# Attention in two transformer layers: heads in order, the maximum pass on 32-row strips of the PE array

## The reference

```
scores = jnp.einsum('bhqd,bhkd->bhqk', q, k) / jnp.sqrt(jnp.float32(HEAD_DIM))
scores = jnp.where(causal[None, None], scores, -jnp.inf)
attn = jax.nn.softmax(scores, axis=-1)
out = jnp.einsum('bhqk,bhkd->bhqd', attn, v)
x = x + ga * (out @ W_o)
```

## Time and profile before

| | |
|---|---|
| median of three runs | 1506.66 us |
| span of the profiled execution | 1517.5 us |
| attention of layer 0 (first maximum tile to the last output tile) | 109.8 to 602.8 us |
| attention of layer 1 | 815.9 to 1306.0 us |
| PE busy over the span | 1211.4 us, 80% |
| DVE busy over the span | 951.7 us, 63% |
| ACT busy over the span | 683.7 us, 45% |

### The profile page before, as it was taken

How to read it: one execution, slowest core, us unless ns; L and a number is a source line. 1 busy time by engine, 2 the same in 40 slices (tenths; PEclk the granted TensorE clock), 3 DMA queues, 4 the chain that set the end, 5 groups by cost and what they waited for, 6 DMA issues and landing times. The chain is left out here.

```text
span 1517.5 us, 20983 instructions
## 1 busy us (share of the span) xinstructions
PE 1211.4 (80%) x7346; PEld 524.4 (35%) x7347; DVE 951.7 (63%) x2598; ACT 683.7 (45%) x895; POOL 187.9 (12%) x257
## 2 busy tenths in 40 slices
PE   2917999999799998319553899999989999676984
PEld 2502333333233343207421223233333334444663
DVE  6627888888678772301163788888868775342443
ACT  1302465665566666103230445566656667421331
POOL 4110000000000000344410000000000000054442
PEclk9857999999899999559875899999999999777997
DMA  4154000230502000022216310140120000011113
GB/s 128 31 118 68 16 16 15 39 74 16 67 15 73 3 3 1 22 63 57 76 50 123 52 43 19 35 87 25 26 44 2 3 3 2 1 35 43 47 47 104
DMA packets 41740, 64.10 MB, mean 42 GB/s; under 512 B 5440, under 2 KB 27872, under 8 KB 41328
## 3 DMA queue, kind: packets, MB, share of 16 engines
q1 hardware_dynamic: 37328, 53.95, 16.4%
q0 software_dynamic: 4320, 8.92, 1.7%
HBM read 45.55 MB, written 18.92 MB: 42 GB/s over the span
## 5 line engine op out<-in xcount | busy, mean ns | idle before, releaser
L792 ACT ACTIVATE probs_at<-st 128x1024 f32<-128x1024 f32 (+3 forms) x640 | 545.7, 897 | 382.4 <-PE st L747 236.4
L810 DVE TENSOR_REDUCE mxp_at<-mx 128x1 f32<-128x512 f32 x768 | 498.4, 685 | 96.0 <-PE mx L716 95.1
L716 PE MATMUL mx<-ks,qs 128*128 128x512 bf16 (+3 forms) x1280 | 379.9, 368 | 84.9 <-DVEq L801 33.2
L747 PE MATMUL st<-qs,ks 128*128 128x512 bf16 (+3 forms) x1280 | 355.6, 354 | 13.9 <-DMA qs<-shrow_at 12.6
L812 DVE CUSTOM_DVE_ANT_0 junk_at<-mx,maskN 128x384 f32<-128x384 f32 (+3 forms) x512 | 241.2, 485 | 104.7 <-PE mx L716 102.4
L763 PE MATMUL av<-probs_at,vs 128*32 128x512 f32 (+3 forms) x2560 | 301.7, 543 | 0.2
L716 PEld LDWEIGHTS mx<-ks,qs 128*128 128x128 bf16 x1280 | 104.8, 98 | 437.7 <-DVE mxp_at L810 183.6
L747 PEld LDWEIGHTS st<-qs,ks 128*128 128x128 bf16 x1280 | 123.4, 99 | 111.0 <-ACT probs_at L792 21.8
L1027 POOL DMA_INDIRECT perm<-rows,pos x64 | 63.3, 989 | 512.6 <-SPq L1136 248.4
L750 PE MATMUL st<-maskTb,identb 128*128 128x128 bf16 x512 | 100.9, 222 | 0.0
L763 PEld LDWEIGHTS av<-probs_at,vs 128*32 128x32 f32 x2560 | 50.6, 108 | 107.2 <-issue 96.7
(11 more groups left out here) (232 smaller groups left out, 1027.8 us busy)
## 6 DMA issues: line engine op xcount, KB each, us to landing
qs<-q_parts SPq DMA_DIRECT2D x63, 128.0 KB
ks<-k_parts SPq DMA_DIRECT2D x18, 384.0 KB
w_sb<-in_w_dram SPq DMA_DIRECT2D x16, 256.0 KB, 3.1
q_parts<-part_pj SPq DMA_DIRECT2D x12, 256.0 KB, 3.0
k_parts<-part_pj SPq DMA_DIRECT2D x12, 256.0 KB, 4.7
perm<-in_pad_dram SPq DMA_DIRECT2D x1, 2600.0 KB, 11.6
rows_f<-perm SPq DMA_DIRECT2D x39, 65.0 KB, 1.8
ks<-k_parts SPq DMA_DIRECT2D x12, 192.0 KB
```

Of the source, the lines that this page charges most:

```text
L716: pe.matmul(buf[:, 0:w], QS[p][:, j, (4 * Q + qb) * P:(4 * Q + qb + 1) * P], KS[p][:, j, c * CH:c * CH + w], start=True, stop=True).then_i ...
L747: mm = pe.matmul(st[half][:, y, off:CH], KS[p][:, j, kb * P:(kb + 1) * P], QS[p][:, j, Q * CH + off:(Q + 1) * CH], start=True, stop=True, ...
L792: act.activation(probs[:, s % 2, 2 * half:2 * half + 2, off:CH], st[half][:, :, off:CH], ACT.Exp, scale=SCALE).then_inc(exp_done[half], 1)
L810: ins = v.tensor_reduce(dst, buf[:, 0:w], AX.X, ALU.max)
```

## The change

The maximum pass no longer uses all 128 rows. The layout of `QS` and `KS` is made anew for each head of a group: head j has its own 32 rows, 32j to 32j+31, with four of the nine products (hi and mid of q with hi and mid of k), and another 40 rows with the other five, followed by 2 shift rows. A maximum tile is a matmul over the 32 rows of one head, at its own row position in the array, so that up to four heads' tiles lie on different strips; the order within a unit now has the head innermost. The scores still use all rows. `MXBUF` stays 3 and `st` stays two double buffers; `probs` has three buffers in place of two; the buffers of maxima and shifts fall from four to two.

`UNITS` now goes head group by head group. `schedule()` has a new model that lets scores run up to three steps ahead of the values, tracks four strips, and orders ACT as well (`ACT_ORDER`). The copy of the turned maxima and of the turned attention moves from DVE to ACT. The shift rows of a unit are four transfers in place of one, a group's load is 12 + 16 transfers in place of 10 + 3, and the ones and zeros that were sent from HBM are written once by POOL.

```diff
-SHIFT0 = 96
+RT = P // GH
+AUX = (RT, 2 * RT, 0, 0)
+SHIFT = [a + 5 * HD for a in AUX]
 MXBUF = 3
+STBUF = 2
+PB = 3
...
-UNITS = [(0, 0), (0, 1), (0, 2), (1, 1), (0, 3), (1, 2), (1, 3), (1, 0),
-         (2, 2), (2, 3), (3, 3), (2, 1), (3, 1), (2, 0), (3, 0), (3, 2)]
+UNITS = [(0, Q) for Q in (0, 1, 2, 3)] + [(1, Q) for Q in (1, 2, 3, 0)] + [(2, Q) for Q in (1, 2, 3, 0)] + [(3, Q) for Q in (3, 2, 1, 0)]
...
+    maxes = [(u, (g, Q, j, qb, c)) for u, (g, Q) in enumerate(UNITS) for qb in range(TPC) for c in range(Q + 1) for j in range(GH)]
...
+        if s < NST and ready[UNIT[s]] is not None and s < a + PB:
+            found.append((max(pe, ready[UNIT[s]] if STEPS[s][2] == 0 else 0., exp_done[half] + lat, all_rows) - .1, "scores"))
+        if a < NST and probs_ready[a] is not None:
+            found.append((max(pe, probs_ready[a] + lat, all_rows, av_free + lat if STEPS[a][2] == 0 else 0.), "values"))
+        if k < len(maxes) and loaded[maxes[k][1][0]] is not None:
+            found.append((max(pe, rows[maxes[k][1][2]], free[b] + lat, loaded[maxes[k][1][0]]) - .05, "max"))
...
-                    for z, rows in enumerate(m.QS + m.KS):
-                        g.memset(rows[64:P].bitcast(F32), 0.).then_inc(m.sem("pool_set"), 1)
-                        g.wait_ge(m.sem("pool_set"), 4 + z + 1)
+                    for p in range(2):
+                        g.memset(m.QS[p][:].bitcast(F32), 0.).then_inc(m.sem("pool_set"), 1)
+                        g.memset(m.KS[p][:], 1.).then_inc(m.sem("pool_set"), 1)
...
-    for a in range(3):
-        r = 3 * a * HD
-        sp.dma_start(m.KS[p][r:r + 3 * HD, :, cols], bass.AP(
-            dram[f"k_parts{L}"].tensor, g * GH * 3 * HD * T + cols.start, [[T, 3 * HD], [3 * HD * T, GH], [1, n]])).then_inc(done, 16)
+    for j in range(GH):
+        at = lambda a: ((g * GH + j) * 3 + a) * HD * T + cols.start
+        src = lambda a, ap: bass.AP(dram[f"k_parts{L}"].tensor, at(a), ap + [[1, n]])
+        to = lambda r, w: m.KS[p][r:r + w, j, cols]
+        sp.dma_start(to(RT * j, 2 * HD), src(0, [[0, 2], [T, HD]])).then_inc(done, 16)
+        sp.dma_start(to(RT * j + 2 * HD, 2 * HD), src(1, [[0, 2], [T, HD]])).then_inc(done, 16)
+        sp.dma_start(to(AUX[j], 2 * HD), src(0, [[T, 2 * HD]])).then_inc(done, 16)
+        sp.dma_start(to(AUX[j] + 2 * HD, 3 * HD), src(2, [[0, 3], [T, HD]])).then_inc(done, 16)
...
-                        sp.dma_start(QS[g % 2][SHIFT0:SHIFT0 + 2 * GH, :, Q * CH:(Q + 1) * CH],
-                                     shrow[:, u % 4, :].unsqueeze(1).to_broadcast([2 * GH, GH, CH])).then_inc(shift_set[u % 4], 16)
+                        for j in range(GH):
+                            sp.dma_start(QS[g % 2][SHIFT[j]:SHIFT[j] + 2, j, Q * CH:(Q + 1) * CH],
+                                         shrow[2 * j:2 * j + 2, n % 2, :]).then_inc(shift_set[n % 2], 16)
...
-                        pe.matmul(buf[:, 0:w], QS[p][:, j, (4 * Q + qb) * P:(4 * Q + qb + 1) * P],
-                                  KS[p][:, j, c * CH:c * CH + w], start=True, stop=True).then_inc(mx_ready, 1)
+                        pe.matmul(buf[:, 0:w], QS[p][strip, j, (TPC * Q + qb) * P:(TPC * Q + qb + 1) * P],
+                                  KS[p][strip, j, c * CH:c * CH + w], start=True, stop=True, tile_position=(RT * j, 0)).then_inc(mx_ready, 1)
...
+                    if half == 0 and SB + s >= PB:
+                        act.wait_ge(av_done, SB + s - PB + 1)
```

More of the change, by code:

```diff
@@ L89, in schedule @@
-    k = s = half = 0
-    lat = 0.1
-    ready = [1e9] * NU
-    free = [0.0] * MXBUF
-    last_max, exp_done = {}, [0.0, 0.0]
-    loaded = [0.0, 22.0] + [1e9] * NG
-    norms = []
+    maxes = [(u, (g, Q, j, qb, c)) for u, (g, Q) in enumerate(UNITS) for qb in range(TPC) for c in range(Q + 1) for j in range(GH)]
+    last_max = [max(k for k, (x, _) in enumerate(maxes) if x == u) for u in range(NU)]
+    lat, rate = .15, 2370.
+    pe = dve = act = 0.
+    rows = [0.] * GH
+    free = [0.] * MXBUF
@@ L659, in attention, with released @@
         late_half = min(u for u, x in enumerate(UNITS) if x[0] == 0 and x[1] >= NC4 // 2)
+        first_of = [min(u for u, x in enumerate(UNITS) if x[0] == g) for g in range(NG)]
+        def released(k):
+            return mx_free[k % MXBUF], L * USES[k % MXBUF] + k // MXBUF + 1
         with nc.Block() as block:
```

390 lines of the change are left out of this document (195 added, 195 removed).

## The result

The changed kernel takes 1681.97 us, the median of four runs between 1673.92 and 1685.17, against 1507.94 us for the kernel before on the same chip. The ratio is 1.1128, with a 95% interval of 1.1081 to 1.1174. It is slower, as forecast, but by 170 us by the ratio (174 between the two medians) where 82 were forecast, and it lies outside the range.

What follows compares the result with a forecast made beforehand. PE was taken to bound the attention, DVE next; steps, joins, start, end and waits summed to 512 us, 530 with the clock, so +37 and +40, plus 5 outside: +82, about 1588 us, range 1555 to 1625.

Steps and rivals of the forecast that it cites:

- start to the first values: Start of each attention, up to its first values: 18 us, as in the kernel before.
- 96 off-diagonal steps: Attention steps away from the diagonal, each with a batch of three strips: 2.32 us each, 223 us per attention.
- 48 diagonal intervals: Attention steps on the diagonal, values to values: mean 1.7 us, 82 us per attention.
- joins without late shift rows: Between units: 99 us of lone tiles, 52 us around them, 19 us for seven short joins, per attention.
- slow clock: After each of nine tile runs PE starts at 1.2 GHz, losing 2 us: 18 us per attention, bounds 0 and 30.
- Waits for transfers: Shift rows of three units queued behind a group load: 4.5 us each, between 0 and 8.2, 13 us per attention.
- The transfers ahead of the attentions: 16 key loads instead of 3 ahead of the projection's last store: 4.6 us in layer 0, 0.4 in layer 1.
- The term for the memsets: POOL's larger memsets come before it has work, costing nothing; under 10 us if that cover failed.
- The strips: Row-strip maximum tiles in steps: a batch of three overlaps, taking 0.24 us, plus 0.09 for each of two mode changes.
- Rival (a): Strips in the attention steps don't overlap, or entering them costs 0.2 us: 1658 us; chance 0.13.
- (b): Strips pay: free mode changes and faster buffer release, off-diagonal steps at 2.1 us, no slow clock: 1491 us; chance 0.12.
- (c): Tile runs cost as forecast, but the clock holds and no shift rows are late: 1527 us; chance 0.17.

Runs made afterwards that it cites:

- e17: Changed kernel, same 28 transfers and bytes per group load, source dimensions turned so 8 or 16 rows come first and the repeat second: ratio 1.0542 to the kernel before.
- e3: Changed kernel's new orders and three probs buffers only, with the earlier kernel's whole-array maximum tiles, layout and 13 load transfers: ratio 1.0556 to the kernel before.
- e6: New orders with whole-array tiles and old layout, but a group load in 29 transfers by head and shift rows in four: ratio 1.0797 to the kernel before.
- e5: Changed kernel with a whole-array matmul ahead of each maximum tile of the nine long runs: ratio 1.1238 to the kernel before.
- e9: Changed kernel with whole-array maximum tiles in place of strips, and four small zeroing transfers more per load: ratio 1.1226 to the kernel before.

## Why the prediction was wrong

By its own steps, each beside what was measured in layer 0 and layer 1:

| step | forecast | layer 0 | layer 1 |
|---|---|---|---|
| start to the first values | 18 | 20.9 | 30.3 |
| 96 off-diagonal steps | 223 | 234.7 | 236.5 |
| 48 diagonal intervals | 82 | 78.2 | 80.4 |
| joins without late shift rows | 170 | 177.6 | 178.5 |
| late shift rows in the joins | 13 | 44.8 | 40.3 |
| slow clock | 18 | in the rows above | in the rows above |
| end of the stretch | 6 | 6.3 | 5.8 |
| attention | 530 | 562.6 | 571.9 |

Between the two profiled spans the kernel grew by 160 us, 78 more than forecast: 59 of these stand in the row of the late shift rows, 15 in the starts, 4 outside the attentions, and the other rows cancel.

**The step that failed is "Waits for transfers".** It had the place right: the group load stands ahead of the shift rows of units (0, 1), (1, 2) and (2, 2). It had the size wrong, 4.5 us each where 10.2 to 17.3 were measured, because it kept "the load's 27.6 us" of the old kernel for a load that is made in another way. Measured in the same way, from the load's first issue to the score behind it (120.26 to 147.85 there), these loads take 36.8 to 38.8 us. That is 9 to 11 us more at each of three joins, about all that the term lacked. It took one load for another since the bytes are nearly the same. With the sources turned (e17), the load is short, the long waits at these three joins go, and the ratio falls from 1.1128 to 1.0542, 5.9 points or some 88 us: 79 us of late rows in the joins, and the rest mostly the load of q ahead of layer 0's attention, which starts at 113.1 in place of 120.4. The price of a late transfer was known to lie within 0 and 8.2 us only as long as the load was the old one; that bound did not hold either.

**The transfers ahead of the attentions** had 0.38 us each, the old ones' price (the product took 0.36). They take 0.63 on average (16 in 10.1 us). Layer 0's attention starts 10.6 us later and not 4.6, by three things: 6.1 us are the projection's, behind the memsets; from the first load of q to that of the keys, which waits for a store of k's parts, it takes 21.1 us where it took 24.2; and from there to the first tile 15.6 where it was 7.9. The term for the memsets failed: they do come before POOL has other work, but DVE, which the forecast did not ask about, was held until they ended. In the seven traces with the old memsets, e3 and e6 with their new order among them, the first store of q's parts is issued between 66.2 and 67.5 us, in the thirteen with the new ones between 71.4 and 74.2. How a memset holds DVE stands in no row. In layer 1 28 transfers stand ahead of the first shift rows. The forecast had 0.4 us there; the score waits 10.05, against 2.8 in the kernel before. That part stays in e17. Four transfers for the shift rows in place of one leave 0.9 to 1.4 us at every other join, which the forecast did not count: about 9 us in an attention. e6 has these waits too and e3, with one transfer, has not.

**The order's price came out near, partly by luck.** The forecast was +82 in all. The order alone (e3) costs 84, and the changed kernel with its transfers put right (e17) costs 1.0542, about 82 us, with attentions of 526.7 and 531.6 us against the forecast 530. These agree partly by balance: e3's steps of 2.57 us in place of 2.32 are 24 us in an attention, and the forecast's 18 us for the clock, counted apart, happen to stand against them; e17 has strips, which save some 15 us, and pays about as much at the starts and joins for its 28 and 4 transfers.

**The strips** came out at the low end that the forecast took, 0.32 and 0.39 us for a batch of three with the change of mode behind it, against 0.33. Over the 110 batches of three that stand between scores and values in this trace the median is 0.32. "TensorEngine Tiling (Array Packing)" of the Trainium skill, section "Key Properties", has the array drained at a change of mode. The trace agrees: four scores from 349.56 on, at 0.215 us each, end at 350.42, and the first strip starts at 350.53. Steps of 2.29 and 2.36 us, near the 2.28 of the sum, leave no room for much more than the 0.09 us charged. Rival (a), whose 1658 us are nearest to what was measured, is refuted by the same rows: its time was near by chance. So is (b), which asked for steps under 2.1 us.

**The clock.** Its fall was forecast and came, to 0.83 and 0.81 on average. What it costs was not settled. Four off-diagonal steps of layer 0 stand in it, with a mean of 3.87 us against 2.38 for the other 92, which is 6 us; five such in layer 1. Steps and joins together are 16 and 20 us over the terms without the clock (12 - 4 + 8 and 13 - 2 + 9), about the forecast's 18, but that sum also holds the 9 us of short waits at the joins, so this agreement is not evidence. e5, which shortened the slow stretches by a quarter to a third, gained nothing, and its filler costs PE time of its own.

**Of the rivals** none described what happened. (c) had no late rows, and e17 shows that without them the kernel still stands at 1.054, not at the 1527 us of (c).

Accounted in points of the ratio, in the order of the runs: order 5.6; a load and the shift rows by head (e6) 2.4; the form and layout of the changed kernel (e9) 4.3; strips -1.0; together 11.3. Of the 6.7 in the middle e17 takes back 5.9 by turning its sources, which leaves 0.8 for the number of transfers and the memsets. How those share was not tried apart. These differences are between runs on several chips, each known to about 0.4 of a point.

## What to carry to other kernels

A transfer's time is no property of its bytes: when its description changes, its duration and its issue have to be taken as unknown and bounded anew, above all where the new source begins with a dimension of 2 or 3. Put the long dimension outermost and a repeat inside. Where short, urgent transfers share an in-order queue with long loads, read who stands ahead of whom in that queue for every unit: the place or the form of the group loads was worth 78 to 88 us here, more than the matmuls' whole form (about 15 us). And when an idle engine is given more to write early on, look at what its neighbours do meanwhile: POOL's larger memsets cost the start some 6 us through DVE.

## What was not expected of the hardware

- 56 plain transfers moved the rows of a load in 19.9 to 21.6 us, 28 with the repeat outermost in 33.6 to 35.5, 28 with it inside in 19.2 to 20.1.
- In the load of 28 with the repeat outermost, two or three 4096-byte packets are under way for 84% of the time, of 159 ns each (median).
- SP issues a transfer of 8 or 16 plain rows in mostly 0.29 to 0.42 us, and one whose source has two dimensions for the rows where the destination has one in mostly 0.57 to 0.72. After seventeen transfers of the slow load an issue is held back for up to 2.5 us.
- Strip tiles issued twice, with PE busy for 25.56 of 28.00 us, left the granted clock at 0.61, hardly above the 0.56 of the run with 23.31 us; a whole-array matmul beside each strip, at 27.98 of 29.00 us, gave 0.82.
- Four DVE instructions that take 1.12 us by themselves took 7.29 us beside POOL's memset of 6.94 us, and ended 0.7 us after it.
- In the kernel before, shift rows sent by POOL or ACT cost 1.2 and 1.6%: beside a group load that SP issues at once, the first score comes 12.1 and 8.2 us after the copy, in place of 3.0 with SP sending rows and then load.
